# Layer 3's feed-forward part worked inside its edge sweep, chunk by chunk of 256 nodes

## What is computed

```python
def gatv2(...):                      # 8 heads of 16 features
    xl = x @ W_l + b_l;  xr = x @ W_r + b_r;  ee = edge_attr @ W_e
    m = leaky_relu(xl[src] + xr[dst] + ee, 0.2)
    logits = einsum('eho,ho->eh', m, att)
    exl = exp(logits - segment_max(logits, dst)[dst])
    alpha = exl / (segment_sum(exl, dst)[dst] + 1e-16)
    return segment_sum(xl[src] * alpha, dst) + b_att
h = layer_norm(x + gatv2(...), g1, be1)
ffn = gelu(h @ W1 + b1) @ W2 + b2          # 128 -> 512 -> 128
return layer_norm(h + ffn, g2, be2)
```

## Time and profile before

| | us |
|---|---|
| median of 3 runs | 7462.92 (7456.25 to 7479.82) |
| span of the profiled execution | 5796.6 |
| lies outside the span (median less span) | 1666.3 |
| TensorE busy, share of the span | 4596.1 (79%) |
| GpSimd busy | 3988.9 (69%) |
| VectorE busy | 2702.8 (47%) |
| ScalarE busy | 1216.6 (21%) |

### The profile page before, as it was taken

The page is one execution under the profiler, slowest core; times in us unless marked ns, Lnnn a source line. Parts: engine busy times, 40 slices in busy tenths (PEclk is TensorE's granted clock), DMA queues, the critical chain, the costliest instruction groups (busy, mean ns, idle before and its releaser), DMA issues. The chain is left out here.

```text
span 5796.6 us, 89863 instructions
## 1 busy us (share of the span) xinstructions
PE 4596.1 (79%) x21959; PEld 3153.3 (54%) x21959; DVE 2702.8 (47%) x8105; ACT 1216.6 (21%) x3182; POOL 3988.9 (69%) x4207
## 2 busy tenths in 40 slices
PE   5888888657777776999999977687777758887887
PEld 4777777535556564444444433455555535555555
DVE  4222222321111113677777766555555545555555
ACT  2111111221211211222222258111111111111111
POOL 6777777457777775777777700777777747777775
PEclk9999999975555555999999989666666666666665
DMA  5333333244444443555555510455555534444443
GB/s 151 106 105 105 105 104 104 74 150 106 112 114 107 118 114 90 160 165 165 165 165 164 166 38 24 109 114 114 113 114 115 113 77 107 111 109 110 109 111 78
DMA packets 559823, 663.58 MB, mean 114 GB/s; under 512 B 196431, under 2 KB 390909, under 8 KB 558717
## 3 DMA queue, kind: packets, MB, share of 16 engines
q1 hardware_dynamic: 424909, 382.99, 22.2%
q0 software_dynamic: 134640, 277.80, 21.1%
HBM read 580.95 MB, written 86.19 MB: 115 GB/s over the span
## 5 line engine op out<-in xcount | busy, mean ns | idle before, releaser
L1792 POOL DMA_INDIRECT soft_rows<-table,sources x2496 | 2388.6, 957 | 1128.2 <-issue 737.7
L1422 POOL DMA_INDIRECT sum_rows<-table,sources x832 | 785.7, 944 | 343.9 <-issue 249.6
L1088 POOL DMA_INDIRECT term_rows<-table,sources x832 | 791.4, 951 | 289.4 <-issue 289.4
L1923 PE MATMUL psum<-soft_onehot,soft_message 128*128 128x64 f32 x3328 | 647.6, 358 | 107.1 <-DVE soft_message L2066 105.0
L1923 PEld LDWEIGHTS psum<-soft_onehot,soft_message 128*128 128x128 f32 x3328 | 586.1, 266 | 188.0 <-issue 181.8
L1119 PE MATMUL psum<-term_onehot,term_term 128*128 128x64 f32 x1664 | 403.9, 425 | 188.5 <-DVE sums L1171 176.6
L1464 PE MATMUL psum<-sum_onehot,sum_rows 128*128 128x64 f32 x1664 | 360.4, 391 | 222.7 <-DMA sum_rows<-table,sources 218.4
L1119 PEld LDWEIGHTS psum<-term_onehot,term_term 128*128 128x128 f32 x1664 | 370.7, 328 | 242.1 <-issue 242.0
L1165 DVE TENSOR_TENSOR term_term<-psum,term_rows 128x512 f32<-128x512 f32 x208 | 143.9, 692 | 753.0 <-issue 349.0
L1464 PEld LDWEIGHTS psum<-sum_onehot,sum_rows 128*128 128x128 f32 x1664 | 343.5, 304 | 278.0 <-issue 273.8
L1919 PEld LDWEIGHTS psum<-soft_onehot,soft_weights 128*4 128x4 f32 (+1 forms) x3328 | 284.9, 109 | 305.9 <-issue 293.0
(11 more groups left out here) (277 smaller groups left out, 6619.9 us busy)
## 6 DMA issues: line engine op xcount, KB each, us to landing
soft_onehotT<-onehotsT SPq DMA_DIRECT2D x312, 256.0 KB
soft_onehot<-onehots SPq DMA_DIRECT2D x624, 128.0 KB, 2.1
soft_attrs<-in_ea128T SPq DMA_DIRECT2D x208, 256.0 KB
soft_rows<-table,sources POOLq DMA_INDIRECT x2496
term_attrs<-in_ea64T SPq DMA_DIRECT2D x208, 128.0 KB, 2.8
onehots<-term_onehot SPq DMA_DIRECT2D x208, 128.0 KB
sum_onehot<-onehots SPq DMA_DIRECT2D x208, 128.0 KB, 2.7
onehotsT<-sum_flat SPq DMA_DIRECT2D x208, 128.0 KB
```

Of the source, the lines that this page charges most:

```text
L1088: pool.indirect_dma_start(rows[:, k, t, :], None, io.table0[0:NCH * CN], bass.IndirectOffsetOnAxis(sb.sources[:, g * TPG + t:g * TPG + t + ...
L1422: pool.indirect_dma_start(rows[:, k, t, :], None, io.table1[0:NCH * CN], bass.IndirectOffsetOnAxis(sb.sources[:, g * TPG + t:g * TPG + t + ...
L1792: pool.indirect_dma_start(rows[:, k, t, :], None, table[0:NCH * CN], bass.IndirectOffsetOnAxis(sb.sources[:, g * TPG + t:g * TPG + t + 1], ...
L1923: last = pe.matmul(bank[:, 0:W], message[:, g.slot(4), b, :], onehot[:, k, b], start=b == 0, stop=b == TPG - 1)
```

## The change

Layer 3's sweep gets a function of its own, gatv2_sweep, and soft_sweep keeps layers 3 and 4 of the code's count only. ffn_phase is no longer called here (another path, for graphs whose windows are wide, keeps it and isn't taken with this input). Its work is in the class FfnNodes, by chunks of 256 nodes, with stages at offsets 2 to 24, so that the sweep's steps go on to 248.

Within the sweep, besides:

- head_logits is taken once for a batch of four groups, at the head of the step that follows the batch's last group by one; the four matmuls write partitions 0, 32, 64 and 96 of one bank. So lanes are group x 32 + head, on 128 partitions, the lane bank is single, and z has four places.
- scatter writes even tiles to partitions 0 to 63 and odd ones to 64 to 127; flip_window is two matmuls with "fold", two stacked identities of 64, which flip and add the halves. It stands directly behind scatter.
- the weights are taken out of the lanes by matmuls with quad_pick instead of transposes; init, carry and factors use 128-partition masks.
- the running maximum back and carry_on stand at the end of VectorE's step, behind the node work.
- lane_starts and lane_cont are loaded by four transfers each a batch (one each before); the one-hot pairs have two places instead of four.
- the node work shares one bank and takes tiles of weights that are no longer needed as buffers; gain and shift of the first normalisation are applied per feature while the chunk is flipped.
- preload_act_table(Exp) is issued behind the second pair of gelus and behind the second root.
- 64 steps (16 before) are written out ahead of the loop.

The core of the diff:

```diff
-    soft_sweep(nc, io, sb, 2)
-    ffn_phase(nc, io, sb)
+    gatv2_sweep(nc, io, sb)
...
+class FfnNodes:
...
+    def attention(self, v, c, t):
...
+        v.tensor_scalar(self.den, self.dens, 1e-16, None, ALU.add).then_inc(s.den[k], 1)
...
+        v.reciprocal(self.den, self.den).then_inc(s.inverse[k], 1)
...
+        v.tensor_tensor(heads, heads, self.den.unsqueeze(3).broadcast_to([P, CB, 8, D // 8]), ALU.mult).then_inc(s.ratio[k], 1)
...
+        v.tensor_tensor(kept, self.blocks, kept, ALU.add).then_inc(s.plus_h[k], 1)
...
+        self.norm1.statistics(v, c, kept)
...
+            for q in (2 * half, 2 * half + 1):
+                act.activation(self.gelu[:, q, :], self.bank[:, q % 2 * CN:q % 2 * CN + CN], ACT.Gelu, bias=self.sb.L2_b1[:, q:q + 1]).then_inc(s.gelu[k], 1)
+            if half:
+                act.preload_act_table(ACT.Exp)
...
+    def act_steps(self, act, t):
+        node_steps(act, t, (2, self.stage), (4, self.norm1.take_root), (6, self.normalise1), (7, self.scaled1), (8, self.gelus(0)), (9, self.gelus(1)),
+                   (12, self.copy_res), (13, self.norm2.take_root), (13, lambda act, c, t: act.preload_act_table(ACT.Exp)), (14, self.normalise2), (19, self.norm3.take_root), (20, self.normalise3),
+                   (21, self.copy_h), (22, self.rows_out))
+
+    def pe_steps(self, pe, t):
+        node_steps(pe, t, (3, self.to_nodes), (7, self.flip_hh), (8, self.ups(0)), (9, self.ups(1)), (10, self.down), (12, self.flip_res),
+                   (21, self.flip_h), (22, self.project))
+
+    def dve_steps(self, v, t):
+        node_steps(v, t, (3, self.attention), (5, self.norm1.scale_shift), (10, self.residual), (12, self.statistics2), (13, self.norm2.scale_shift),
+                   (15, self.to_x), (19, self.norm3.scale_shift))
...
+    FIRST = 4 * AROUND
+    LAST = STEPS * (NCH - 1 + BEHIND) + 24
...
+                    nodes.act_steps(act, t)
+                    g = t.back(LAG)
+                    if g.exists():
+                        act.wait_ge(s.scattered, g.times(1, 1))
+                        wait_past(act, s.window_T, g, 1, 0)
+                        act.activation(window, window_bank, ACT.Copy).then_inc(s.window_copied, 1)
...
+                def head_logits(g):
+                    pe.wait_ge(s.leaky, g.times(1, BATCH))
...
+                    for j in range(BATCH):
+                        last = pe.matmul(lane_bank[j * QUAD:(j + 1) * QUAD], sb.att_cols, z[:, j], start=True, stop=True)
...
+                        last = pe.matmul(window_bank[b % 2 * W:b % 2 * W + W], onehot[:, k, b], message[:, g.slot(2), b, :], start=b < 2, stop=b >= TPG - 2)
...
+                    pe.matmul(window_T[:, 0:W], window[:, 0:D], fold, start=True, stop=True)
+                    pe.matmul(window_T[0:H, P:P + W], window[:, D:D + H], fold, start=True, stop=True).then_inc(s.window_T, 1)
+
+                def step(t):
+                    if t.back(BATCH).closes(0):
+                        head_logits(t.back(BATCH))
+                    if t.exists():
+                        edge_terms(t)
+                    nodes.pe_steps(pe, t)
...
+                    g = t.back(LAG)
+                    if g.exists():
+                        scatter(g)
+                        flip_window(g)
...
+                    if t.exists():
+                        edge_sum(t)
+                    nodes.dve_steps(v, t)
+                    if t.back(BATCH + 1).closes(0):
+                        running_back(t.back(BATCH + 1))
+                        carry_on(t.back(BATCH + 1))
```

More of the change, by code:

```diff
@@ L42 @@
 BATCH = 4
+QUAD = P // BATCH
 LAG = BATCH + 3
@@ L1659, in soft_sweep @@
+    spread = {3: sb.lane_expand4, 4: sb.ones}[layer]
     mask, heads = sb.lane_mask[0:L], sb.lane_head[0:L, 0:H]
     AHEAD = 4
-    DST = AHEAD if full else BATCH
     phase = f"soft{layer}"
-    FIRST = AROUND if full else 4 * AROUND
-    LAST = G + LAG if full else STEPS * (NCH - 1 + BEHIND) + 14
-    names = ("order cleared starts_in cont_in rows_T rows_out edge_term z leaky src_out logits lanes_out running backward fend carry_psum carry shift init_psum init maxima "
-             "shifted factor_log weights_lane factor spread weights_T weights_out factor_psum factor_out columns message "
-             "scattered window_copied window_T").split()
@@ L1668, in soft_sweep @@
-    s = sems(nc, phase, *names, gathered=AROUND, attr=AHEAD, dst_rows=DST, onehotT=4, onehot=4)
+    FIRST = 4 * AROUND
+    LAST = STEPS * (NCH - 1 + BEHIND) + 14
+    names = ("order cleared starts_in cont_in edge_term leaky src_out logits lanes_out running backward fend carry_psum carry shift init_psum init maxima "
+             "shifted factor_log weights_lane factor spread weights_T weights_out factor_psum factor_out message "
+             "scattered").split()
+    s = sems(nc, phase, *names, gathered=AROUND, dst_rows=BATCH, onehotT=4, onehot=4)
@@ L1711, in soft_sweep @@
         factor_head_bank = sb.psum[0:H, 7, 48:48 + BATCH]
-        nodes = None if full else GatNodes(nc, io, sb, tile, layer, sb.psum[:, 2, :])
-        CLEARED = 4 + (not full)
+        nodes = GatNodes(nc, io, sb, tile, layer, sb.psum[:, 2, :])
+        CLEARED = 5
         ORDER = 4
@@ L1809, in step @@
                 def step(t):
-                    if not full and t.back(BATCH).closes(0):
+                    if t.back(BATCH).closes(0):
                         take_sources(t.back(BATCH))
@@ L1846, in step @@
                     if g.closes(0):
-                        act.wait_ge(s.logits, g.times(1, BATCH) if full else g.uses(BATCH))
+                        act.wait_ge(s.logits, g.uses(BATCH))
                         if g.back(BATCH).exists():
@@ L1899, in src_logits @@
                     last.then_inc(s.logits, 1)
-                def scatter(g):
-                    k = g.slot(4)
-                    wait_past(pe, s.window_copied, g, 1, 0)
-                    pe.wait_ge(s.onehot[k], g.uses(4, 16))
-                    pe.wait_ge(s.columns, g.times(1, 1))
-                    pe.wait_ge(s.message, g.times(1, 1))
-                    for b in range(TPG):
-                        last = pe.matmul(window_bank, onehot[:, k, b], message[:, g.slot(2), b, :], start=b == 0, stop=b == TPG - 1)
-                    last.then_inc(s.scattered, 1)
                 def scatter_T(g):
@@ L1942, in step @@
                     if g.exists():
-                        (scatter if full else scatter_T)(g)
-                    if full and t.back(1).exists():
-                        head_logits(t.back(1))
-                    if not full and t.back(BATCH).closes(0):
+                        scatter_T(g)
+                    if t.back(BATCH).closes(0):
                         src_logits(t.back(BATCH))
-                    if g.exists() and full:
-                        flip_window(g)
                     g = t.back(BATCH + 1)
```

699 lines of the change are left out of this document (574 added, 125 removed).

## The result

The changed kernel takes 7526.02 us (median of four runs, 7523.89 to 7534.46), the kernel before beside it 7464.61: a ratio of 1.008, 95% interval 1.006 to 1.0101, or +61 us. The forecast was +154 us: right in sign and too large by a factor of 2.5.

A forecast was written before the change was run, and what follows sets the result against it. TensorE's full queue was taken to bound the sweep at 5.12 us a group, GpSimd allowing 5.0. 309 - 10 + 10 - 155 = +154 us on 7462.9 gave 7617, range 7400 to 7790.

The forecast's parts named there:

- The drain: Chunk work left after the last edges replaces the feed-forward phase between sweeps: 95 us for 250, a gain of 155.
- The sweep: Layer 3's edge sweep with nodes: 55.2 us for eight groups against 41.0, 21.75 rounds, 309 us more.
- 1666 us lie outside the profiled span: Whole kernel: span 5796.6 us against median 7462.9, the difference placed outside the span and taken as unchanged.
- the walk: Step-by-step count of layer 3's sweep, from edge term to edge term: 50.6 + 2h = 55.2 us for eight groups.
- another time outside the span: Whole kernel: a listed sign that the forecast is wrong, beside a period below 6.0 or a low granted clock.
- rival 4: TensorE's clock falls in the sweep: at 0.85, 5 us more a round, +110, 7725; chance 0.28 with rival 3.
- The eight intervals: Times between ends of successive edge terms in one round of the new sweep: sum 50.6 + 2h = 55.2 us.
- h: A batch's four head-logit matmuls on TensorE: 2.3 us with partial overlap; low end 1.1, high end 3.9.
- rival 3: Column tiles in head logits and scatter don't overlap: 59 us a round, +95, 7710; chance 0.28 with rival 4.
- Rebuilt sweep without nodes: The sweep's first 34 steps, which have no nodes: 5.4 us instead of 5.12, 10 us more.
- Rival 5: Early exponential table load isn't worth its place or costs nothing: 28 us of the sum, without them 7589; no chance given.
- Rival 1: The sweep's waits hide: eight groups take 44 to 45 us, net -80, 7385; loses above 48 a round; chance 0.17.

The follow-up runs named there:

- c1: The changed kernel unedited, once more, on a 7.5 ms chip: 7600.08 us, 1.0068 of the kernel before.
- e0: The kernel before, unchanged, profiled again on a 7.5 ms chip: 7545.96 us.
- c2: The changed kernel with scatter, then head logits, ahead of the edge terms, message ahead of window sums, window copy ahead of nodes, on a 7.5 ms chip: 7738.91 us, 1.0373.
- e13: The changed kernel with scatter, then head logits, ahead of the edge terms, message ahead of window sums, window copy ahead of nodes, on the 5.8 ms chip: 6423.77 us, 1.1083.
- e2: The changed kernel with VectorE's leaky maximum directly behind the edge sum, ahead of the node work: 7645.25 us, 1.0138.
- e1: The changed kernel's rebuilt sweep without node work, the old feed-forward phase behind it: 7617.42 us, 1.0079 of the kernel before.
- e9: The changed kernel without the early loads of the exponential's table: 7603.91 us, 1.0064 of the kernel before.
- e15: e13 without the early loads of the exponential's table: 6431.15 us, 1.1089 of the kernel before.
- c0: The changed kernel unedited, on the chip of the experiments: 7532.14 us, 1.0101 of the kernel before.
- e5: The kernel before with each of layer 3's 208 edge-attribute matmuls done twice: 7487.9 us, 1.0041.
- e11: The kernel before with layer 3's edge-attribute matmul left out: 7496.91 us, 0.9929.
- e8: The changed kernel with unread matmuls ahead of each window flip and each batch's head logits: 7618.51 us, 1.0083 of the kernel before.
- e14: The kernel before without the matmul and load of layer 3's edge attributes, on the 5.8 ms chip: 5778.52 us, 0.9964.
- e3: The changed kernel with ScalarE's window copy ahead of its node work in the step: 7617.4 us, 1.0076 of the kernel before.
- e6: The changed kernel with each window flipped in the next step, behind that step's four transposes: 7674.72 us, 1.0298 of the kernel before.
- e12: The changed kernel with head logits, transposes and scatter ahead of edge terms, message ahead of window sums, window copy ahead of nodes, on the 5.8 ms chip: 6449.75 us, 1.1113.

## Why the prediction was right in sign and wrong in size

Spans of c1 and e0 (both on chips where the kernel before takes 7.55 ms) differ by 7601.9 - 7543.6 = 58 us: sweep 1724 - 1532 = +192, drain 111 - 248 = -137, rest +3.

**The drain.** Forecast 95 for 250, a gain of 155; measured 111 for 248, 137. The mechanism held, and the size within its bounds (75 to 115).

**The sweep.** Forecast +309; measured +192. Two errors of opposite sign lie in it.

First, the base. The step that failed is "1666 us lie outside the profiled span ... I take them as unchanged": they lie inside, in all sweeps, 451 of them in this one. From the 35th group on the old sweep runs at (1532 - 292) / 173 x 8 = 57.3 us a round, not 41.0. (In its own profile it is 41.7: the rounds are 41.1 and 42.3 to 42.6 in turn, and the walk has the shorter one.) The new waits stand where pauses and the low clock behind them stood, so that only the difference is paid: the changed kernel is at (1724 - 299) / 173 x 8 = 65.9, +8.6 instead of +14.2. That one takes the place of the other is read from c2 and e13, which keep 75 us on either kind of chip, and from e2, where pauses come back with a wait taken out; no run shows how. The prediction did name "another time outside the span" as a sign of being wrong. But a span that is 22% short of the median should not have been explained by time outside, of which no row showed anything; it should have been carried as a rival.

Second, the clock, rival 4. The eight intervals in the round at 3762.58 (measured between starts of the destination terms), forecast and measured: 9.3 and 10.4; 5.1 and 6.8; 4.4 and 5.0; 7.0 and 8.7; 9.0 and 10.1; 5.4 and 5.9; 6.8 and 8.3; 8.2 and 10.1. The sum is 65.1 for 55.2. Six pieces of transposes and terms at 4.07 instead of 2.49 us are 9.5 us, nearly all of it. Rival 4 put 5 us on a round at a clock of 0.85; it is 0.79 and twice as much. The waits themselves are 13.6 us, where the walk had them: 5.0 for the leaky, 7.2 for the window (8 x 0.5, and more behind gelus), 1.4 for the weights. One was not in it: every second round the leaky wait is 5.1 instead of 2.0, where the loop of 16 steps turns, and such rounds take 68 us instead of 65.

Had only the base been right, with the walk at 55.2, the forecast would have been 21.6 x (55.2 - 57.3) - 155: a gain of some 200. The clock alone is 21.6 x 9.5 = 205 us, the base 21.6 x (57.3 - 41.0) = 352: each is larger than the result, and that the time came near the forecast is luck, owed to their opposite signs.

**Head logits.** h was taken as 2.3 with bounds 1.1 and 3.9. The four matmuls take 1.00 us at the upper level (e1) and 1.87 at the lower (3768.38 to 3770.25), against 4 x 0.98 one by one: four tiles of 32 columns overlap wholly, and rival 3 is out. (Its +95 fits 1.2 us more on each batch of the first 34 steps, not on each step as it says, which would be +124.) The Trainium skill ("TensorE: Matmul & The Clock Gate", Part 3) has 2.38 times for three column tiles; here it is 3.9 for four. The scatter with two tiles of 64 is 0.6 for 1.06.

**Rebuilt sweep without nodes.** Forecast 0.28 us a group, which over 208 groups is 58 us; e1 has 68 in the sweep. The agreement is chance, since e1's own 7.5 us a group is not the forecast's 5.4.

**Table load.** Rival 5 said that it might cost nothing; e9 and e15 bear that out. A load is 1.28 us and the next operation starts 0.01 behind its end; c0's ScalarE:

```profile
3478.11 1.28 ACT L1799 ACT_TABLE_LOAD   x1 [3.71 <-PE psum L1788]
3479.40 0.84 ACT L1799 ACTIVATE soft_gelu<-psum,L_b 128x256 f32<-128x256 f32 x2
```

As in the earlier trace rows, nothing is seen of the 1.38 us of drain that the Trainium skill ("ScalarE: Activation LUTs", What ACT_TABLE_LOAD costs) adds.

**Rival 1** (waits hide) had its point of decision at 48 us a round; with the base at 57.3 the point is 57.3 + 137 / 21.6 = 63.6, and the kernel missed it by 2.3 us. No variant of the changed kernel came below the kernel before either.

**Open.** What makes TensorE pause on the 7.5 ms chips. The runs show that the old sweep's pace there doesn't follow TensorE's work (e5, e11), that the pauses fade where nodes are in the steps and come back where a wait is taken out or filled (e2, e8), and that the 5.8 ms chip has none. Whether transfers have a part wasn't settled, since e14 fell on the other kind.

One thing points at GpSimd. At the start of this sweep it issues 64 gathers back to back, 80 us long, on either kind of chip. On the 5.8 ms chip ScalarE copies transposed rows as soon as TensorE is done; in e0 it starts the third copy 9 us late, the next two 26 us late each, and is on time again only behind the 64 gathers. Its program waits there for nothing but these transposes and head logits that are done by then. So the first eight groups take 103 us, from the first attribute term to the ninth, instead of 43. The third transposes and their copy, in the profile of the earlier trace rows, then in e0:

```profile
2302.01 0.97 PE L1867 MATMUL psum<-ident,soft_rows 128*128 128x128 f32 x4
2303.01 0.60 ACT L1829 ACTIVATE soft_z<-psum 128x512 f32<-128x512 f32 x1 [6.49 <-PE psum L1867]
```

```profile
2852.18 1.12 PE L1867 MATMUL psum<-ident,soft_rows 128*128 128x128 f32 x4
2862.54 0.60 ACT L1829 ACTIVATE soft_z<-psum 128x512 f32<-128x512 f32 x1 [15.91 <-DMA sum_onehot<-onehots]
```

Between 3200 and 4200 us of e0, 35 of 137 window copies start over 2 us behind their scatter. All 35 scatters end while GpSimd issues a run of four or eight gathers, and 28 of the copies start 0.6 to 1.9 us behind the last of these gathers. That is no proof: 96 scatters that are copied in time end inside such runs too, and no run changed the gathers.

## What to carry to other kernels

Before a single row is costed, set the profile's span beside the median: if they differ by more than a few per cent, the profile shows another execution than the one that is timed, and the pace of each stage must be taken as unknown between the two. A wait put into a full TensorE queue can cost itself and the lower clock behind it; here a round with 13.6 us of waits also has some 9.5 us of slower matmuls, though filling 4 us of the waits (e8) won nothing back. And taking a wait out of a ring of three engines won nothing in any of five tries (e2, e3, e6, e12, e13): waits or pauses came back at another place, so the order of the whole step has to be walked, not one edge of it.

## What the runs showed of the hardware

- Two kinds of chip: the same program in 5799 us and in 7440 to 7570 us, with GpSimd's gather at 944 to 947 ns median on both. The difference is idle time and granted clock of TensorE: VectorE's message takes 669 ns and ScalarE's copy of the rows 597 ns on both.
- Work added to TensorE can be nearly free: in the old sweep on a 7.5 ms chip 212 us of matmuls cost 31 us, and the granted clock is 0.94 where e0 has 0.85.
- On a 7.5 ms chip ScalarE can see TensorE's work as done 26 us late while GpSimd issues gathers without a break (e0, 2864 to 2918 us); on the 5.8 ms chip the same stretch shows no delay.
- Four fp32 matmuls into four column tiles of 32 take the time of one (1.00 for 3.9 us).
